# Ratios of dequantisation scales computed behind the turned rows of the first unit instead of ahead of the statistics of the moved rows

## What is computed

```
xn = layernorm(x)
# attention, 32 query heads on 8 key/value heads, head size 128, weights of 4 bits
w   = (qw - 8) * repeat(scales, 128, axis=0)        # for q, k, v and o
q, k, v = xn @ wq, xn @ wk, xn @ wv;  q, k = rope(q), rope(k)
ctx = softmax(causal(q k^T / sqrt(128))) @ v
attn = ctx @ wo
# a linear layer with 8 low-rank experts (rank 16), the two best by a router
p = top2(softmax(xn @ W_router.T));  p = p / sum(p)
ffn = xn @ W_base.T + b_base + 2 * sum_e p_e * (xn @ A_e.T) @ B_e.T
out = x + attn + ffn
```

## Time and profile before

| | |
|---|---|
| median of 3 runs | 1868.37 us (1861.88 to 1869.31) |
| profiled execution | 1870.37 us, span 1868.60 us |
| TensorE (PE) busy | 1775.9 us, 95% |
| VectorE (DVE) busy | 1520.5 us, 81% |
| ScalarE (ACT) busy | 1307.0 us, 70% |
| GpSimd (POOL) busy | 1153.7 us, 62% |
| mean granted TensorE clock | 0.983 |
| chain that ended last | PE 59%, DMA 14%, DVE 11%, POOL 7%, issue 4% |

### The profile page before, as it was taken

How to read it: one execution, slowest core, us unless ns; L and a number is a source line. 1 busy time by engine, 2 the same in 40 slices (tenths; PEclk the granted TensorE clock), 3 DMA queues, 4 the chain that set the end, 5 groups by cost and what they waited for, 6 DMA issues and landing times.

```text
span 1868.6 us, 29198 instructions
## 1 busy us (share of the span) xinstructions
PE 1775.9 (95%) x9578; PEld 1490.7 (80%) x9580; DVE 1520.5 (81%) x3082; ACT 1307.0 (70%) x2775; POOL 1153.7 (62%) x1085
## 2 busy tenths in 40 slices
PE   8898999999999999999899999999999999999987
PEld 6787787887878887887778778888778888788776
DVE  6758788788878888788876889878887889778875
ACT  3237777678766887677676677778676777768764
POOL 1236577667685677666665476856767667766653
PEclk8999999999999999999999999999999999999999
DMA  5406445454554545544763745534454445534453
GB/s 192 153 17 147 113 128 139 118 135 108 136 130 123 137 118 138 130 117 104 199 168 91 198 144 134 147 108 136 117 139 125 119 123 137 150 99 130 114 159 106
DMA packets 284623, 244.18 MB, mean 131 GB/s; under 512 B 32660, under 2 KB 213944, under 8 KB 284472
## 3 DMA queue, kind: packets, MB, share of 16 engines
q1 hardware_dynamic: 281160, 236.54, 47.0%
q0 software_dynamic: 2112, 4.19, 0.8%
q10 hardware_dynamic: 1200, 1.59, 0.3%
HBM read 164.40 MB, written 77.86 MB: 130 GB/s over the span
## 4 chain that ended last, share of the span: by engine, by line
PE 59%; DMA 14%; DVE 11%; POOL 7%; issue 4%; SPq 3%; ACT 3%; POOLq 0%; DVEq 0%
PE ring L1892 16%; PE O_ps L1737 16%; PE ring L1827 8%; PE ring L1828 8%; PE ring L1737 7%; DMA squares<-probs 4%; PE ring L1903 3%; POOL moved_low L1184 2%; DMA raw<-in_qw_o 2%; DMA moved<-squares 2%; DVE rope L1582 2%; DVE ctx_f L1633 2%; DMA stage<-in_scales_v 2%; SPq L1004 2%; DMA R_sb<-row_sums 2%
## 5 line engine op out<-in xcount | busy, mean ns | idle before, releaser
L1341 ACT ACTIVATE ring<-ring,ratios 128x512 f32<-128x512 f32 x736 | 465.3, 666 | 107.8 <-PE ring L1828 99.9
L1326 ACT ACTIVATE probs<-probs,negmax 128x128 f32<-128x128 f32 (+7 forms) x512 | 394.3, 772 | 101.5 <-DVE negmax L1598 100.3
L1598 DVE CUSTOM_DVE_ANT_0 probs<-ring,mask_row 128x128 f32<-128x128 f32 (+7 forms) x512 | 372.2, 749 | 47.0 <-PE ring L1892 44.6
L1184 POOL TENSOR_TENSOR moved_low<-moved,moved_high 128x512 fp32r<-128x512 f32 x256 | 326.4, 1290 | 73.4 <-ACT moved_high L1249 69.2
L1220 POOL TENSOR_TENSOR ctx_low<-ctx_f,ctx_high 128x512 fp32r<-128x512 f32 x128 | 165.3, 1291 | 247.1 <-ACT ctx_high L1249 246.3
L1249 ACT ACTIVATE PT_high<-ring 128x512 fp32r<-128x512 f32 (+3 forms) x515 | 222.0, 442 | 131.0 <-PE ring L1903 119.1
L1474 DVE TENSOR_TENSOR PT_low<-ring,PT_high 128x512 fp32r<-128x512 f32 (+3 forms) x515 | 245.9, 484 | 77.3 <-ACT PT_high L1249 60.9
L1191 POOL TENSOR_TENSOR rope<-rope 128x512 f32<-128x512 f32 x160 | 206.8, 1292 | 148.3 <-DVE rope L1582 129.8
L1827 PE MATMUL ring<-xnT_high,W 128*128 128x512 f32 x640 | 267.2, 417 | 1.6 <-ACT ring L1341 1.2
L1892 PE MATMUL ring<-K_high,Q_high 128*128 128x512 f32 (+3 forms) x768 | 240.9, 368 | 14.6 <-DVE PT_low L1474 6.8
L1828 PE MATMUL ring<-xnT_low,W 128*128 128x512 f32 x640 | 251.8, 393 | 0.0
(11 more groups left out here) (149 smaller groups left out, 3724.0 us busy)
## 6 DMA issues: line engine op xcount, KB each, us to landing
squares<-probs SPq DMA_DIRECT2D x256, 256.0 KB, 2.4
moved<-squares SPq DMA_DIRECT2D x256, 256.0 KB, 4.9
R_sb<-row_sums SPq DMA_DIRECT2D x128, 256.0 KB, 3.7
raw<-in_qw_q SPq DMA_DIRECT2D x64, 256.0 KB, 3.6
raw<-in_qw_o SPq DMA_DIRECT2D x64, 256.0 KB, 5.3
raw<-in_qw_k SPq DMA_DIRECT2D x16, 256.0 KB, 2.8
raw<-in_qw_v SPq DMA_DIRECT2D x16, 256.0 KB, 2.7
stage<-in_scales_v SPq DMA_DIRECT2D x16, 256.0 KB, 4.6
```

Source lines behind the costliest of these rows:

```text
L1184: nc.gpsimd.tensor_tensor(out=low, in0=moved[:, :, j, :], in1=high.bitcast(f32), op=ALU.subtract).then_inc(moved_done, 1)
L1326: nc.scalar.activation(probs[:, at], probs[:, at], ACT.Exp, bias=negmax[:, i:i + 1], scale=-1.0, accum_out=sums[:, i:i + 1]).then_inc(exp_ ...
L1341: nc.scalar.activation(place(step), place(step), ACT.Copy, scale=ratio(step)).then_inc(rescaled, 1)
L1598: nc.vector.tensor_tensor_reduce(row, ps, hidden_keys, -1.0, -MASKED, ALU.add, ALU.min, negmax[:, i:i + 1]).then_inc(negmax_ready, 1)
```

## The change

In the VectorE program, `scale_ratios()` is called behind `low("turn_x", 0, 6)`, the low part of the seventh turned tile of batch 0, instead of behind `linear_read(1, 3)`. In `awaited`, the load of the first value weights now depends on `low("turn_x", 0, 7)`, the eighth. No instruction is added or taken away.

```
@@ awaited, kind "load" @@
             if at[1] == "va" and not u:
-                out.append(("linear", PARKED, 3))
+                out.append(("low", "turn_x", STARTED[1], NT - 1))
@@ vector program, behind low(*s) @@
                     elif s[0] == "turn_x" and s[1] != PARKED and s[2] + 2 < NT:
                         normalise(s[1], s[2] + 2)
+                    elif s == ("turn_x", STARTED[1], NT - 2):
+                        scale_ratios()
@@ vector program, behind linear_read(*of) @@
                     b, t = of
-                    if b == PARKED and t == 3:
-                        scale_ratios()
                     if b == PARKED and t in (3, 5):
```

## The result

The changed kernel took 1874.09 us, the median of 16 runs (1868.62 to 1882.67). The kernel before, in as many runs on the same chip, took 1863.01 us (1854.8 to 1871.9). The ratio is 1.0051, with a 95% interval of 1.0029 to 1.0072: slower by about 9.5 us (the medians lie 11.1 us apart), where 1867.4 and no measurable change were forecast.

A forecast was written before the change was run, and what follows sets the result against it. TensorE, busy 1775.9 of 1868.6 us, was taken as the bound. Opening gain 2.8 - 1.8 = 1.0 us, new order at nothing: profiled 1870.37 to 1869.4, or 1867.4 against the median 1868.37; range 1858 to 1877.

The forecast's parts named there:

- Part 1: Opening: 5.58 us of ratios leave VectorE's old place, GpSimd's value weights leave too; `lora_a` 0 starts 5.9 us earlier.
- Part 2: Opening, new place: ratios run 76.4 to 82.0, `lora_a` 7 starts at 82.75; 2.8 of 5.9 us are left.
- Part 3: TensorE ahead of `lora_a` 7: 4.6 us idle, low clock behind costs 1.8 us; gain left 1.0, from 0 to 2.8.
- nothing is left of it: Opening: the low clock lasts longer and takes the whole 2.8 us, giving 1868.4; chance 0.23.
- Parts 4 and 5: Opening: `base` still sets `turn_hidden`, routing has 2.25 us to spare; later value loads cost nothing, 12 us to spare.
- Part 6: Main part: new order changes TensorE's waits; middle at nothing, usual size 6 us, ends +18 and -16 us.
- The order waits more for moved tiles: Main part: value products wait longer behind GpSimd's low parts, up to 18 us, 1885; chance 0.16 for over 10 us.
- The order waits less: Main part, value products behind GpSimd's low parts: 16 us less waiting gives 1851; chance 0.13 for over 8 us.
- The ratios are wholly hidden: Opening, new place on VectorE: the full 5.9 us stay, giving 1862.5; chance 0.02.
- Value weights come late: Value products: GpSimd or loads 12 us slower than before, each further microsecond costing one; chance 0.01.

The follow-up runs named there:

- The order alone: Kernel before with only the plan's dependency of the first value load changed, ratios in their old place: 1874.09 us against 1864.87, ratio 1.0059.
- the filled kernel: Changed kernel with 18 matmuls of zeros in TensorE's idle gap ahead of `lora_a` 7: 1867.12 us against 1864.87 for before, ratio 1.0010.
- four hybrids: Ratios in old place, before's and new order joined at 780 or 1050 us of the plan's clock: ratios 1.0039, 1.0048, 1.0060, 1.0055 against before.
- three of altered costs: Kernel before with one planner cost altered: add 0.68, value weight 4.0 or norm 1.0; ratios 1.0062, 1.0074, 1.0011 against before.
- the "norm" order: Kernel before with the plan's cost of a norm at 1.0 instead of 0.99: 1868.16 us, ratio 1.0011.
- the kernel with the place alone: Before's order kept, ratios in their new place, two value loads set behind the parking of `Y`: 1860.4 us against 1864.87, ratio 0.9983.

## Why the prediction was wrong

**What bounds the kernel.** Right: TensorE, in its waits and its clock.

**Part 1.** Right. The statistics start at 50.58, which is 52.6 on before's scale (with the offset of 1.97). The two normalisings take 1.00 us and a single one 0.54 instead of 1.60, GpSimd being quiet. The turns and the 27 matmuls from 60.08 on run without a gap. The order alone, which keeps GpSimd away too and leaves the ratios, gains 2.1 us in the opening.

**Part 2.** Right. The ratios run from 74.48, which is 76.4, to 80.02, which is 82.0; `lora_a` 7 stands at 80.68 for 82.75 - 1.97 = 80.78 forecast.

**Part 3.** The gap was right, 4.51 us for 4.6. Its price was mis-sized: taken was 1.8 us, read off windows of 5.5 and 4 us; measured was 3.3, in the 60 matmuls behind the gap and again in the filled kernel. The window of 4 us had been closed too early. Behind the gap of 3.17 us the lower clock goes on to 1083.2, which is 3.0 us lost and no longer near 1.8:

```profile
1077.20:1083.20 6.00, 6.00 (x16) 4.84 (x17) 5.30 (x11) 0.66 (x2) 5.84 (x6) 0.50 0.94 308
```

The upper end of 2.8 was too low as well, as the low clock can cost more than what it is set against. The opening therefore loses 0.4 us instead of gaining 1.0. The rival "nothing is left of it" was the better forecast of the opening, but these 1.4 us are small beside the loss of 9.5. The rule of the Trainium skill (TensorE: Matmul & The Clock Gate, section HAM oscillation) that long idle gaps bring the lower clock back held here, with 0.50 in the row behind the gap.

**Parts 4 and 5.** Right. `turn_hidden` follows `base` directly, 15.82 us behind `lora_a` 7, and value weights are ready at 95.49 + 1.30 = 96.8, some 14 us ahead of the value products at 110.88.

**Part 6.** This step failed. It put the middle of the new order "at nothing, as nothing in the rows favours a side". The order alone costs 0.59% of 1864.87, some 11 us, against a usual size of 6; as its opening is 2.1 us shorter, its main part loses some 13. The mechanism named for either side, waits for moved tiles, was wrong too: they became shorter by 6.3 us. What failed is the symmetry, as far as is known. Of the eight orders tried that differ from before's (the new one, four hybrids, three of altered costs), only the "norm" order was not clearly slower, and none was faster. Four of the eight are not independent, but together they speak for an order of before that is better than most others of this planner. A draw of a new order is thus a draw against a good one; that the middle was put at nothing came from rows of one order alone. Nor does one kind of wait bound what an order costs: the waits for moved tiles became shorter and the kernel slower. Why the new plan is longer stays open; part of the loss is granted clock, part length at full clock.

**The rivals.** "The order waits more for moved tiles" had the right sign, the 18 us of its upper end were twice the size, and its mechanism is refuted. "The order waits less" fell with the order alone. "The ratios are wholly hidden" is refuted by the 4.51 us gap, and shown to be reachable by cutting them up. "Value weights come late" did not happen.

## What to carry to other kernels

An edit of one dependency in a planner's input is two edits: the one meant, and a new plan everywhere; build the meant one with the old order kept, and judge the order by itself. Here only naming the eighth low part changed the order: with the seventh, behind which the ratios really stand, the planner gives before's order step for step on TensorE, VectorE, ScalarE and GpSimd, with before's PSUM banks, and on SyncE it moves the two loads just to where the kernel with the place alone has them. Small work moved out of the path should be cut to the length of the idle stretches it moves into: 15 instructions in one block cost a gap of 4.5 us and 3.3 us of clock, and in five pieces they left no gap, and the kernel was 0.53% faster than before (0.17% faster in one block, not clear of noise).

## What the runs showed of the hardware

A gap of 4.51 us was followed by 7.0 us at 0.50 of the clock. The time at the lower level, and not the gap, was the surprise: with 18 matmuls of zeros in the gap, which left 0.62 us of it open, the clock stayed at 1.00 and 3.3 us came back.

Normalising 128x512 took 0.54 us with GpSimd idle and 1.60 beside its value weights, while the statistics took 2.87 us for four and reads from PSUM 0.75 us in both cases.

The mean granted clock of one kernel on one core varied between executions, from 0.977 to 0.988 over 16 runs of the changed kernel, and times went with it (correlation -0.69). The span multiplied by that clock spread less for the kernel before (2.8 us against 6.5, standard deviations of 35 runs) and not less for the changed kernel (4.5 against 4.0 in 16 runs). By it the order alone, in 12 runs, lay 4.7 us from before with an error of 0.9.
